# One of the four dBx products per scan state goes from VectorE to GpSimd, fed by a ScalarE copy of the B row

## The chip, the cores and the metric
One NeuronCore of a Trainium2 chip runs the whole program. The metric is the device time of one execution in microseconds (us), lower is better.

## The reference
The kernel computes two adaLN layers on 1024 tokens of width 512: a selective scan (Mamba style) with a routed LoRA feed-forward, then attention with an ALiBi bias and a quantised gated feed-forward. The change lies in the scan alone:

```
A   = -exp(A_log)                                  # 512 channels x 16 states
xp  = x @ x_proj_w.T ;  dt_in, B, C = split(xp)    # 16 | 16 | 16 per token
dt  = softplus(dt_in @ dt_proj_w.T + dt_proj_b)
dA  = exp(dt * A)
dBx = dt * B * x
h_t = dA_t * h_{t-1} + dBx_t                       # over 1024 tokens
y_t = sum over the 16 states of h_t * C_t ;  y = y + D * x
```

## The kernel before
Channels lie on the 128 partitions, in four blocks c = 0..3; tokens lie along the free dimension and are done in two halves h of 512. Within a half the 16 states follow one another; N = 16h + n counts them through. A helper, scan_turns, gives every engine the same loop: the first pair of states written out, six pairs in a hardware loop, the last pair written out (o = 0, 1 is the state within the pair). The engines are ordered by semaphores only, each in the order of its own program. For one state:

- TensorE broadcasts the row B (L623, PSUM bank 5) and the row C (L627, bank 4) of 512 tokens over all partitions. In its program the two broadcasts for state N+1 stand behind the hC matmul of channel block 0 of state N and ahead of that of block 1 (L645 to L650). The hC matmuls (L649, f32, against an identity, each recorded as two) add hC up over the states in banks 0 to 3. The broadcast of B waits until VectorE has done all four dBx products of the state before, that of C until C has been copied.
- ScalarE copies C to SBUF (L492, C_sb, two buffers), then computes dA of the four blocks as an exponential (L496) into banks 6 and 7 in turn; the exponential of block c waits for the scan that freed its bank, two blocks earlier.
- VectorE forms dBx = u * B of each block (L986, u from SBUF, B from PSUM, dBx to SBUF), one block ahead of the scan, and scans the block: hs = dA * hs + dBx (L1006). In its order: dBx c+1, scan c. In the first half of the tokens it also copies the last column of hs to a small tile, state (L990, keep_state); in the second half the scan starts from that.
- GpSimd multiplies hC = hs * C (L410), a block at a time, behind the scan. It waits for the hC matmul of the state before, which frees the buffer.

A scan of block c writes over hs of the state before, so it waits for GpSimd's hC of that block (`hc_done`).

Of the kernel before, what the change touches and what calls it, by code (L numbers as in the profile page):

```python
# [18 lines left out]
P = 128  # L19
# [72 lines left out]
def program(nc, a, out):  # L92
    ctx = ExitStack()
    with ctx:
# [60 lines left out]
        sp_exp = at("sp_exp", RG + 8, [P, DC, HALF])  # L155
        sp_w = at("sp_w", RG + 16, [P, DC, HALF])
        dBx = at("dBx", RG + 8, [P, DC, HALF])
        hs = at("hs", RG, [P, DC, HALF])
        hC = at("hC", RG + 16, [P, DC, HALF])
        C_sb = at("C_sb", RG + 24, [P, 2, HALF])  # L160
# [62 lines left out]
        for n in ("in_c in_x in_id in_misc in_l0 in_lf in_attn in_proj in_gate in_up in_down wd_p0 wd_p1 wd_p2 wd_r0 wd_r1 in_att "  # L223
                  "c_exp c_silu mod_acc mod_prod mod_mm mod_done mod_rest negA setup "
                  "ln_ve ln_rstd ln_norm ln_tr ln_hT "
                  "xp_mm xp_dt xp_bc dt_mm sp_e sp_w sp_act sp_lo sp_dve sp_free "
                  "b_mm c_mm c_evac da_done dbx_done scan_done st_done hc_done sum_done y_done ym yt "
                  "x0 ar_mm r_soft r_exp hw_done hw_tr hw_evac f0_mm f0_y x1 x1pre bias0 "
                  "qk_mm qk_evac qk_split v_mm v_done "
                  "s_mm m_done r_part rec_done r_rdy rt_mm rt_evac st_mm exp_done pv_done ot_evac ot_tr ao_done v_ones "  # L230
                  "aot_tr aot_evac pj_mm pj_y x2 x2pre bias1 "
                  "g_mm f_exp f_sgn f_y0 f_out dn_mm dn_y0 dn_sgn dn_y dn_done out_dma dchain pchain achain").split():
            sem(n)
# [128 lines left out]
        @block.gpsimd  # L362
        def _(pool):
            n = [0]

            def link(ins):
                n[0] += 1
                ins.then_inc(S["pchain"], 1)
                pool.wait_ge(S["pchain"], n[0])

            pool.memset(ones[:], 1.0).then_inc(S["setup"], 1)
            pool.memset(zb[:], 0.0).then_inc(S["setup"], 1)
            pool.memset(state[:], 0.0).then_inc(S["setup"], 1)
            link(pool.memset(mhalf[:], -0.5))

            def ln_rstd(l, h):
                pool.wait_ge(S["ln_ve"], 2 * l + h + 1)
                pool.tensor_tensor(rstd[:, 4 * h:4 * h + 4], veps[:, 4 * h:4 * h + 4], mhalf[:, 0:4], ALU.pow) \  # L378
                    .then_inc(S["ln_rstd"], 1)

            def pre_add(l, s, row):
                for t in range(NT):
                    pool.wait_ge(S["ln_norm"], NT * l + t + 1)
                    pool.tensor_tensor(x_tok[:, t, :], x_tok[:, t, :], row, ALU.add).then_inc(S[s], 1)

            ln_rstd(0, 0)
            ln_rstd(0, 1)

            for i in range(2 * DC):
                h, c = i // DC, i % DC  # L390
                if c == 0:
                    for c_ in range(DC):
                        pool.wait_ge(S["sp_e"], DC * h + c_ + 1)
                        pool.tensor_tensor(uT[:, c_, half(h)], sp_exp[:, c_, :], uT[:, c_, half(h)], ALU.subtract) \
                            .then_inc(S["sp_lo"], 1)
                pool.wait_ge(S["sp_dve"], i + 1)
                link(pool.tensor_tensor(dtT[:, c, half(h)], dtT[:, c, half(h)], sp_log[:, c, :], ALU.add))
                pool.tensor_tensor(uT[:, c, half(h)], dtT[:, c, half(h)], hT[:, c, half(h)], ALU.mult) \
                    .then_inc(S["sp_free"], 1)
            pool.wait_ge(S["sp_free"], 2 * DC)  # L400

            def scan(h, m, first_, last):
                for o in range(2):
                    N = m * 2 + (16 * h + o)
                    pool.wait_ge(S["c_evac"], N + 1)
                    for c in range(DC):
                        pool.wait_ge(S["scan_done"], N * DC + (c + 1))
                        if not (first_ and o == 0):
                            pool.wait_ge(S["sum_done"], N * DC + (c - 3))
                        pool.tensor_tensor(hC[:, c, :], hs[:, c, :], C_sb[:, o, :], ALU.mult) \  # L410
                            .then_inc(S["hc_done"], 1)

            scan_turns(pool, scan)
            ln_rstd(1, 0)
            ln_rstd(1, 1)
            pool.wait_ge(S["bias0"], 16 * 5 + 1)
            pre_add(1, "x1pre", bbc[:])

            pool.wait_ge(S["mod_prod"], 2)
            link(pool.tensor_tensor(wmod[:, 0, :], wmod[:, 0, :], wmod[:, 1, :], ALU.add))  # L420
            pool.wait_ge(S["mod_prod"], DC)
            link(pool.tensor_tensor(wmod[:, 2, :], wmod[:, 2, :], wmod[:, 3, :], ALU.add))
            pool.tensor_tensor(wmod[:, 0, :], wmod[:, 0, :], wmod[:, 2, :], ALU.add).then_inc(S["mod_acc"], 1)
            ln_rstd(2, 0)
            ln_rstd(2, 1)
            pool.wait_ge(S["x1"], NT)
            pool.memset(V[:, :, :, HD:32], 1.0).then_inc(S["v_ones"], 1)
            pool.wait_ge(S["bias1"], 16 * 2 + 1)
            pre_add(2, "x2pre", bpc[:])

            ln_rstd(3, 0)
            ln_rstd(3, 1)

            for i in range(IC + 1):
                for part, k in ((0, i), (1, i - 1)):
                    if 0 <= k < IC:
                        M = M_of(k)
                        pool.wait_ge(S[f"wd_p{part}"], k + 1)
                        pool.tensor_tensor(wd[0:M, k, :], wd[0:M, k, :], wdp[0:M, part, k, :], ALU.subtract) \
                            .then_inc(S[f"wd_r{part}"], 1)  # L440
# [3 lines left out]
        def _(act):  # L444
# [38 lines left out]
            act.wait_ge(S["sp_free"], 2 * DC)  # L483
            act.wait_ge(S["negA"], 2)

            def scan(h, m, first_, last):
                for o in range(2):
                    N = m * 2 + (16 * h + o)
                    act.wait_ge(S["c_mm"], N + 1)
                    if not first_:  # L490
                        act.wait_ge(S["hc_done"], N * DC - 4)
                    A_(C_sb[:, o, :], ps[:, C_BANK, :], ACT.Copy).then_inc(S["c_evac"], 1)  # L492
                    for c in range(DC):
                        if not (first_ and o == 0 and c < 2):
                            act.wait_ge(S["scan_done"], N * DC + (c - 1))
                        A_(ps[:, DA_BANK + c % 2, :], dtT[:, c, half(h)], ACT.Exp,  # L496
                           scale=nA[:, bass.ds(m * 2 + (o + c * NS), 1)]).then_inc(S["da_done"], 1)

            scan_turns(act, scan)
            ln_out(1, 0, 3, 4)  # L500
# [75 lines left out]
        def _(pe):  # L576
# [42 lines left out]

            def broadcast(h, n, guarded):  # L620
                if guarded:
                    pe.wait_ge(S["dbx_done"], n * DC + 16 * h * DC)
                mm(ps[:, B_BANK, :], sel[:, bass.ds(n, 1)].to_broadcast([96, P]), BCs[:, half(h)],  # L623
                   start=True, stop=True).then_inc(S["b_mm"], 1)
                if guarded:
                    pe.wait_ge(S["c_evac"], n + 16 * h)
                mm(ps[:, C_BANK, :], sel[:, bass.ds(n + NS, 1)].to_broadcast([96, P]), BCs[:, half(h)],  # L627
                   start=True, stop=True).then_inc(S["c_mm"], 1)
# [240 lines left out]
        def _(v):  # L869
# [109 lines left out]
            def scan(h, m, first_, last):  # L979
                def driven(o, c):  # L980

                    N = m * 2 + (16 * h + o)
                    v.wait_ge(S["b_mm"], N + 1)
                    if not (first_ and o == 0):
                        v.wait_ge(S["scan_done"], N * DC + (c - 3))
                    tt(dBx[:, c, :], uT[:, c, half(h)], ps[:, B_BANK, :], ALU.mult).then_inc(S["dbx_done"], 1)  # L986
# [9 lines left out]
                for o in range(2):  # L996
                    N = m * 2 + (16 * h + o)
                    for c in range(DC):
                        if not (last and o == 1 and c == DC - 1):
                            driven(o + (c + 1) // DC, (c + 1) % DC)  # L1000
                        v.wait_ge(S["da_done"], N * DC + (c + 1))
                        v.wait_ge(S["dbx_done"], N * DC + (c + 1))
                        if not (first_ and o == 0):
                            v.wait_ge(S["hc_done"], N * DC + (c - 3))
                        init = 0.0 if h == 0 else state[:, bass.ds(m * 2 + (o + c * NS), 1)]
                        v.tensor_tensor_scan(hs[:, c, :], ps[:, DA_BANK + c % 2, :], dBx[:, c, :], init,  # L1006
                                             ALU.mult, ALU.add).then_inc(S["scan_done"], 1)
                        if before and h == 0:
                            keep_state(*before)
                        before = (o, c)  # L1010
# [307 lines left out]
```

## Time and profile before
| | us |
|---|---|
| median of 3 runs | 1123.4 (1119.11 to 1123.93) |
| the profiled execution | 1121.76 |
| its span | 1120.0 |
| first half of the scan | about 118 to 242 |
| second half of the scan | about 255 to 371 |

Over the whole span TensorE's matmuls are busy 878.5 us (78%), VectorE 832.2 (74%), ScalarE 418.6 (37%), GpSimd 283.3 (25%). These shares are means over stages with different limits. In the rows below PE is TensorE's matmul, PEld its weight load, DVE is VectorE, ACT is ScalarE, POOL is GpSimd. An instruction's name is its source line with what it writes and reads. A start and an end come from the hardware profiler; the ends of matmuls are modelled.

### The profile page before, as it was taken

The numbers are of one execution on the slowest core, as the hardware profiler recorded it, in microseconds if no ns is written. First come the engines' busy times: TensorE is split into PE (matmuls) and PEld (weight loads), VectorE is DVE, ScalarE is ACT, GpSimd is POOL, SyncE is SP. The second block draws the span as 40 slices with busy tenths as digits, with TensorE's granted clock in tenths as the row PEclk, the third lists the DMA queues.
The fourth block names the chain that finished last, engine by engine and source line by source line (L and its number), as shares of the span: only waits on it lengthen the run. The fifth ranks groups of instructions, "written<-read, shape, count | busy, mean of one in ns | idle before, by whom it ended". The sixth has DMA issues, their size and how long they took to land.

```text
span 1120.0 us, 12563 instructions
## 1 busy us (share of the span) xinstructions
PE 878.5 (78%) x4157; PEld 404.6 (36%) x4166; DVE 832.2 (74%) x1307; ACT 418.6 (37%) x691; POOL 283.3 (25%) x210
## 2 busy tenths in 40 slices
PE   1750577656766583879759999999998889999997
PEld 1320122222111361434335555555544344444443
DVE  5299899989999757629359887778740639976777
ACT  0421344424444150022100666666675045543300
POOL 1135566645777290113000000000000014400000
PEclk9855699998999886979969999999999999999999
DMA  9314000000000000413420122222005000000010
GB/s 358 123 49 176 1 0 0 0 0 1 0 0 0 17 1 0 148 27 127 147 79 19 57 65 65 65 65 63 6 2 195 8 1 0 1 0 1 1 38 37
DMA packets 28797, 54.37 MB, mean 49 GB/s; under 512 B 7956, under 2 KB 14868, under 8 KB 27592
## 3 DMA queue, kind: packets, MB, share of 16 engines
q1 hardware_dynamic: 28744, 53.68, 14.2%
q8 instruction: 31, 0.51, 0.2%
q14 instruction: 22, 0.18, 0.1%
HBM read 45.08 MB, written 8.39 MB: 48 GB/s over the span
## 4 chain that ended last, share of the span: by engine, by line
PE 52%; DVE 9%; SPq 2%; issue 2%; ACT 1%; DMA 1%; POOL 0%; DVEq 0%; POOLq 0%
PE ps L852 14%; PE ps L776 7%; PE ps L758 5%; PE ps L863 5%; PE ps L740 3%; PE ps L745 3%; PE ps L834 2%; PE ps L795 2%; SPq L267 2%; PE ps L583 1%; PE ps L761 1%; PE ps L678 1%; PE ps L743 1%; PE ps L672 1%; DVE qkf L1125 1%
## 5 line engine op out<-in xcount | busy, mean ns | idle before, releaser
L532 ACT ACTIVATE prob<-ps 128x512 f32<-128x512 f32 x288 | 160.3, 600 | 141.1 <-PE ps L761 113.3
L649 PE MATMUL ps<-hC,identf 128*128 128x512 f32 x256 | 151.6, 682 | 73.8 <-POOL hC L410 72.3
L410 POOL TENSOR_TENSOR hC<-hs,C_sb 128x512 f32<-128x512 f32 x128 | 162.4, 1270 | 94.0 <-DVE hs L1006 73.3
L378 POOL TENSOR_TENSOR rstd<-veps,mhalf 128x4 f32<-128x4 f32 x8 | 10.4, 1294 | 459.0 <-DVE veps L890 459.0
L496 ACT ACTIVATE ps<-dtT,nA 128x512 f32<-128x512 f32 x128 | 88.2, 690 | 101.6 <-DVE hs L1006 101.6
L1142 DVE TENSOR_REDUCE mrow<-ps 128x4 f32<-128x512 f32 x160 | 103.1, 686 | 23.4 <-PE ps L743 12.2
L758 PE MATMUL ps<-stack 123*128 123x512 bf16 (+3 forms) x384 | 113.0, 327 | 0.6 <-ACT prob L532 0.3
L649 PEld LDWEIGHTS ps<-hC,identf 128*128 128x128 f32 x256 | 42.3, 201 | 166.9 <-POOL hC L410 163.7
L1145 DVE TENSOR_REDUCE mrow<-ps 128x1 f32<-128x512 f32 x128 | 82.0, 685 | 24.7 <-PE ps L745 24.7
L986 DVE TENSOR_TENSOR dBx<-uT,ps 128x512 f32<-128x512 f32 x128 | 86.6, 678 | 7.4 <-PE ps L623 4.8
L740 PE MATMUL ps<-stack 120*128 120x128 bf16 x640 | 73.8, 222 | 19.7 <-DVE mrow L1142 16.3
L852 PE MATMUL ps<-hT,wg 128*128 128x512 f32 (+1 forms) x176 | 80.9, 603 | 3.0 <-ACT hT L463 3.0
L1006 DVE TENSOR_TENSOR_SCAN hs<-ps,state,dBx 128x512 f32<-128x512 f32 x64 | 82.5, 1291 | 0.0
L776 PE MATMUL ps<-prob,V 128*32 128x512 f32 (+3 forms) x768 | 81.6, 498 | 0.7 <-ACT prob L532 0.7
L852 PE MATMUL ps<-hT,wu 128*128 128x512 f32 (+1 forms) x176 | 79.1, 592 | 0.0
L1006 DVE TENSOR_TENSOR_SCAN hs<-ps,dBx 128x512 f32<-128x512 f32 x64 | 77.9, 1218 | 0.3 <-ACT ps L496 0.3
L740 PEld LDWEIGHTS ps<-stack 120*128 120x128 bf16 x640 | 51.6, 99 | 62.7 <-DVE mrow L1142 37.9
L463 ACT ACTIVATE hT<-ps,modc 128x512 f32<-128x512 f32 x32 | 22.3, 776 | 109.4 <-PE ps L583 99.3
L710 PE MATMUL ps<-hT,wattn 128*128 128x512 f32 x128 | 58.8, 620 | 3.5 <-ACT hT L463 3.0
L863 PE MATMUL ps<-wdp,inter 128*128 128x512 bf16 (+1 forms) x258 | 56.7, 379 | 0.3
L583 PE MATMUL ps<-identf,xn 128*128 128x128 f32 x128 | 25.4, 374 | 32.6 <-DVE xn L897 32.5
L852 PEld LDWEIGHTS ps<-hT,wg 128*128 128x128 f32 (+1 forms) x176 | 33.5, 191 | 45.8 <-issue 45.8
(185 smaller groups left out, 1366.6 us busy)
## 6 DMA issues: line engine op xcount, KB each, us to landing
wmod<-in_wmod SPq DMA_DIRECT2D x8, 1536.0 KB, 13.6
stack<-parts_dram SPq DMA_DIRECT2D x192, 64.0 KB
parts_dram<-qkp SPq DMA_DIRECT2D x48, 128.0 KB, 1.8
wattn<-in_wattn SPq DMA_DIRECT2D x1, 3072.0 KB, 13.3
wg<-in_wg SPq DMA_DIRECT2D x1, 2752.0 KB, 9.3
wu<-in_wu SPq DMA_DIRECT2D x1, 2752.0 KB, 10.7
wd<-in_wd SPq DMA_DIRECT2D x1, 2560.0 KB, 12.7
x_tok<-in_x SPq DMA_DIRECT2D x1, 2048.0 KB, 8.0
```

Source lines behind the costliest of these rows:

```text
L410: pool.tensor_tensor(hC[:, c, :], hs[:, c, :], C_sb[:, o, :], ALU.mult) \
L496: A_(ps[:, DA_BANK + c % 2, :], dtT[:, c, half(h)], ACT.Exp, scale=nA[:, bass.ds(m * 2 + (o + c * NS), 1)]).then_inc(S["da_done"], 1)
L532: A_(prob[:, u % 4, j, :], ps[:, 3 + F % 3, :], ACT.Exp).then_inc(S["exp_done"], 1)
L649: mm(ps[:, c, :], identf[:], hC[:, c, :], start=False, stop=False, skip_group_check=True).then_inc(S["sum_done"], 1)
L740: ins = mm(ps[:, bank, tile(j_)], qk[0:ATT_S, 0, j_, tile(i)], qk[0:ATT_S, 1, j_, tile(kb)], start=True, stop=kb < i)
L758: ins = mm(ps[:, bank, col:col + w], qk[0:ATT_ALL, 1, j, tile(kb)], qk[0:ATT_ALL, 0, j, q0:q0 + w], start=True, stop=not diag)
L776: ins = mm(ps[32 * j:32 * j + 32, 6 + b, q0 % HALF:q0 % HALF + w], V[:, kb, g * GH + j, :], prob[:, U % 4, j, col:col + w], start=(kb == 0 ...
L852: ins = mm(ps[0:M, 2 * s + b, :], w[:, k, ib * P:ib * P + M], hT[:, k, half(h)], start=(k == 0), stop=(k == DC - 1))
L863: ins = mm(ps[:, 4 + t % 4, :], inter[0:M, k, tile(t)], wdp[0:M, part, k, :], start=(k == 0 and part == 0), stop=(k == IC - 1 and part == 2))
L986: tt(dBx[:, c, :], uT[:, c, half(h)], ps[:, B_BANK, :], ALU.mult).then_inc(S["dbx_done"], 1)
L1006: v.tensor_tensor_scan(hs[:, c, :], ps[:, DA_BANK + c % 2, :], dBx[:, c, :], init, ALU.mult, ALU.add).then_inc(S["scan_done"], 1)
L1142: v.reduce_max(mrow[:, kb, :, i], ps[:, bank, :].rearrange("p (j c) -> p j c", c=P), AX) \
```

## The change
The kernel gets two more SBUF buffers of 128 x 512 f32: a second buffer for the dBx of block 3 (dB3 alternates between it and the old one) and B_sb, a copy of the B row. The steps:

- ScalarE copies the B row of state N+1 from PSUM to B_sb, between its exponentials of blocks 2 and 3 of state N (and the row of state 0 of each half first of all). It waits for the broadcast and until GpSimd has used the row before. It signals `b_evac`.
- GpSimd forms dBx of block 3 of state N+1 from B_sb, between its hC products of blocks 1 and 2 of state N (and that of state 0 of each half first of all). It waits for `b_evac` and signals `dbx3_done`.
- VectorE forms dBx of blocks 0 to 2 only, still from PSUM, but waits for `b_evac` in place of the broadcast. Its order in a state is now dBx 1, scan 0, dBx 2, scan 1, scan 2, dBx 0 of the next state, scan 3.
- TensorE's broadcast of B waits for the three dBx products of the state before and for the copy of its row.

```diff
+        dB3 = [dBx[:, DC - 1, :], at("dB3", RG + 28, [P, HALF])[:]]
+        B_sb = at("B_sb", 30, [P, HALF])
@@ GpSimd
+            def driven(h, N, o):
+                pool.wait_ge(S["b_evac"], N + 1)
+                pool.tensor_tensor(dB3[o], uT[:, DC - 1, half(h)], B_sb[:], ALU.mult).then_inc(S["dbx3_done"], 1)
             def scan(h, m, first_, last):
+                if isinstance(m, int) and m == 0:
+                    if h:
+                        pool.wait_ge(S["scan_done"], 16 * DC)
+                    driven(h, 16 * h, 0)
...
+                        if c == 1 and not (last and o == 1):
+                            driven(h, N + 1, 1 - o)
@@ ScalarE
+            def copy_b(N, read):
+                act.wait_ge(S["b_mm"], N + 1)
+                if read:
+                    act.wait_ge(S["dbx3_done"], N)
+                A_(B_sb[:], ps[:, B_BANK, :], ACT.Copy).then_inc(S["b_evac"], 1)
...
+                        if c == 2 and not (last and o == 1):
+                            copy_b(N + 1, True)
@@ TensorE, broadcast
-                    pe.wait_ge(S["dbx_done"], n * DC + 16 * h * DC)
+                    pe.wait_ge(S["dbx_done"], n * (DC - 1) + 16 * h * (DC - 1))
+                    pe.wait_ge(S["b_evac"], n + 16 * h)
@@ VectorE
-                    v.wait_ge(S["b_mm"], N + 1)
+                    v.wait_ge(S["b_evac"], N + 1)
...
-                        if not (last and o == 1 and c == DC - 1):
-                            driven(o + (c + 1) // DC, (c + 1) % DC)
+                        if c < DC - 2:
+                            driven(o, c + 1)
+                        elif c == DC - 1 and not (last and o == 1):
+                            driven(o + 1, 0)
...
-                        v.wait_ge(S["dbx_done"], N * DC + (c + 1))
+                        if c < DC - 1:
+                            v.wait_ge(S["dbx_done"], N * (DC - 1) + (c + 1))
+                        else:
+                            v.wait_ge(S["dbx3_done"], N + 1)
...
-                        v.tensor_tensor_scan(hs[:, c, :], ps[:, DA_BANK + c % 2, :], dBx[:, c, :], init,
+                        v.tensor_tensor_scan(hs[:, c, :], ps[:, DA_BANK + c % 2, :],
+                                             dBx[:, c, :] if c < DC - 1 else dB3[o], init,
```

## Rows read from the trace of the kernel before

**Rows 1.** Busy time of each engine by stretch; x counts, granted clock, DMA.

```profile
core 0: us, PE busy (x) PEld busy (x) DVE busy (x) ACT busy (x) POOL busy (x), PEclk, DMA share, GB/s
118.00:242.00 124.00, 87.03 (x162) 25.68 (x162) 115.40 (x192) 52.01 (x80) 81.26 (x64) 0.90 0.00 0
...
255.00:371.00 116.00, 80.69 (x158) 22.96 (x159) 113.52 (x128) 50.56 (x78) 81.84 (x65) 0.96 0.00 0
```

**Rows 2.** Groups by line in the scan: busy us, mean ns, idle before, releasers.

```profile
L410 POOL TENSOR_TENSOR hC<-hs,C_sb 128x512 f32<-128x512 f32 x128 | 162.4, 1270 | 94.0 <-DVE hs L1006 73.3 <-issue 18.0 <-PE ps L649 2.8
...
L986 DVE TENSOR_TENSOR dBx<-uT,ps 128x512 f32<-128x512 f32 x128 | 86.6, 678 | 7.4 <-PE ps L623 4.8 <-issue 2.3
...
L1006 DVE TENSOR_TENSOR_SCAN hs<-ps,dBx 128x512 f32<-128x512 f32 x64 | 77.9, 1218 | 0.3 <-ACT ps L496 0.3
...
L492 ACT ACTIVATE C_sb<-ps 128x512 f32<-128x512 f32 x32 | 19.1, 597 | 72.1 <-PE ps L627 58.4 <-POOL hC L410 13.7
```

**Rows 3.** Timeline, second half, one state: start, duration, engine, line, idle before.

```profile
299.13 1.28 DVE L1006 TENSOR_TENSOR_SCAN hs<-ps,state,dBx 128x512 f32<-128x512 f32 x1
...
306.22 1.29 DVE L1006 TENSOR_TENSOR_SCAN hs<-ps,state,dBx 128x512 f32<-128x512 f32 x1
...
307.42 0.67 DVE L986 TENSOR_TENSOR dBx<-uT,ps 128x512 f32<-128x512 f32 x1
...
307.67 1.27 POOL L410 TENSOR_TENSOR hC<-hs,C_sb 128x512 f32<-128x512 f32 x1 [0.57 <-DVE hs L1006]
308.00 1.29 DVE L1006 TENSOR_TENSOR_SCAN hs<-ps,state,dBx 128x512 f32<-128x512 f32 x1
...
309.00 1.12 PE L649 MATMUL ps<-hC,identf 128*128 128x512 f32 x2 [0.72 <-POOL hC L410]
309.19 0.68 DVE L986 TENSOR_TENSOR dBx<-uT,ps 128x512 f32<-128x512 f32 x1
...
310.00 0.39 PE L623 MATMUL ps<-BCs,sel 96*128 96x512 bf16 x1
...
310.96 0.68 DVE L986 TENSOR_TENSOR dBx<-uT,ps 128x512 f32<-128x512 f32 x1
```

**Rows 4.** Timeline of VectorE, first half, around two loop turns.

```profile
193.50 1.22 DVE L1006 TENSOR_TENSOR_SCAN hs<-ps,dBx 128x512 f32<-128x512 f32 x1
...
195.46 0.69 DVE L986 TENSOR_TENSOR dBx<-uT,ps 128x512 f32<-128x512 f32 x1 [0.45 <-issue]
196.07 1.22 DVE L1006 TENSOR_TENSOR_SCAN hs<-ps,dBx 128x512 f32<-128x512 f32 x1
...
210.98 1.22 DVE L1006 TENSOR_TENSOR_SCAN hs<-ps,dBx 128x512 f32<-128x512 f32 x1
```

**Rows 5.** Timeline, end of the first half.

```profile
236.82 1.22 DVE L1006 TENSOR_TENSOR_SCAN hs<-ps,dBx 128x512 f32<-128x512 f32 x1
...
237.99 1.22 DVE L1006 TENSOR_TENSOR_SCAN hs<-ps,dBx 128x512 f32<-128x512 f32 x1
238.12 2.49 POOL L410 TENSOR_TENSOR hC<-hs,C_sb 128x512 f32<-128x512 f32 x2 [0.50 <-DVE hs L1006]
```

**Rows 6.** Timeline, start of the first half, TensorE at half clock.

```profile
118.40 0.63 PE L627 MATMUL ps<-BCs,sel 96*128 96x512 bf16 x1
...
119.15 0.60 ACT L492 ACTIVATE C_sb<-ps 128x512 f32<-128x512 f32 x1 [30.21 <-PE ps L627]
119.64 1.29 ACT L496 ACTIVATE ps<-dtT,nA 128x512 f32<-128x512 f32 x2
120.36 1.22 DVE L1006 TENSOR_TENSOR_SCAN hs<-ps,dBx 128x512 f32<-128x512 f32 x1 [0.34 <-ACT ps L496]
...
121.75 1.27 POOL L410 TENSOR_TENSOR hC<-hs,C_sb 128x512 f32<-128x512 f32 x1 [7.81 <-DVE hs L1006]
...
123.08 2.07 PE L649 MATMUL ps<-hC,identf 128*128 128x512 f32 x2 [4.04 <-POOL hC L410]
...
124.94 0.63 PE L623 MATMUL ps<-BCs,sel 96*128 96x512 bf16 x1
...
125.61 0.69 DVE L986 TENSOR_TENSOR dBx<-uT,ps 128x512 f32<-128x512 f32 x1 [0.50 <-PE ps L623]
```

**Rows 7.** Waits in the scan: total us, times, longest.

```profile
DVE dBx L986 <- PE ps L623: 4.8, 6, 2.6
```

More of the change, by code:

```diff
@@ L226, in program @@
                   "xp_mm xp_dt xp_bc dt_mm sp_e sp_w sp_act sp_lo sp_dve sp_free "
-                  "b_mm c_mm c_evac da_done dbx_done scan_done st_done hc_done sum_done y_done ym yt "
+                  "b_mm c_mm c_evac b_evac da_done dbx_done dbx3_done scan_done st_done hc_done sum_done y_done ym yt "
                   "x0 ar_mm r_soft r_exp hw_done hw_tr hw_evac f0_mm f0_y x1 x1pre bias0 "
@@ L484, in _ @@
             act.wait_ge(S["negA"], 2)
+            def copy_b(N, read):
[3 more added lines that the diff above has]
+                A_(B_sb[:], ps[:, B_BANK, :], ACT.Copy).then_inc(S["b_evac"], 1)
             def scan(h, m, first_, last):
+                if isinstance(m, int) and m == 0:
+                    copy_b(16 * h, h > 0)
                 for o in range(2):
```

## The prediction
> **What bounds the kernel now.** The edit touches nothing outside the two scan stages, so I first read the busy times by stretch, to see who fills these stages. Over the first half VectorE is busy 115.4 of 124 us and GpSimd 81.3; over the second VectorE 113.5 of 116, GpSimd 81.8, ScalarE 50.6 [rows 1]. VectorE is the wall, all others have room. The groups of instructions by line then say what fills it: per state (16 states in each half) four dBx products of 0.68 us and four scans of 1.22; one GpSimd product takes 1.27, a ScalarE copy of a 512-column row 0.60 [rows 2].
>
> Busy times don't say what follows when VectorE gets shorter; for that I walked the timeline of one steady state [rows 3]. State to state, scan of channel 0 to scan of channel 0, is 306.22 - 299.13 = 7.09 us. The reader should see a second path beside VectorE: the B row is broadcast by one TensorE matmul (L623), which stands in TensorE's program behind the hC matmul of channel 0. That matmul needs GpSimd's hC of channel 0, and this needs scan 0 of the same state. The row is there at 310.00 + 0.39 = 310.39 and its first reader, the dBx of channel 0 of the next state, starts at 310.96. So this path has only 0.57 us to spare per state. Everything turns on that number.
>
> **What the change does to VectorE alone.** It removes 32 dBx products. Between two scans a product costs its issue distance: 0.58 (307.42 to 308.00 [rows 3]) or 0.61 us (195.46 to 196.07 [rows 4]); a scan with no product behind it costs 1.17 (236.82 to 237.99 [rows 5]). If nothing else were late, a state would take 7.09 - 0.60 = 6.49, and 32 states would give back 32 x 0.60 = 19 us. VectorE's busy time falls by 32 x 0.68 = 21.8 in any case.
>
> **What it adds on the B path.** ScalarE copies the B row before anybody may read it, and even VectorE's own products now wait for the end of that copy. The path, from GpSimd's start on hC of channel 0:
> - GpSimd hC: 1.27 [rows 2]; to the matmul 0.06 (307.67 + 1.27 = 308.94, 309.00 [rows 3]).
> - hC matmul until the broadcast starts. In the steady row it is 1.00 (309.00 to 310.00), but there the broadcast is released by the dBx of channel 3, which ended at 309.87; that condition goes earlier by the change. The bare distance shows where TensorE ran at half clock: 124.94 - 123.08 = 1.86 [rows 6]; half of it, 0.93, is my value at full clock. The far ends are nothing at all (if it were hidden) and 1.86; the nearest row bounds it at 1.00 from above, and below 0.93 nothing in the rows goes.
> - Broadcast 0.39 [rows 3]; to ScalarE 0.12 (118.40 + 0.63 = 119.03, 119.15 [rows 6]).
> - The copy 0.60 [rows 2]; to its reader 0.03 (exponential 119.64 + 0.69 = 120.33, scan 120.36 [rows 6]).
>
> Sum 1.27 + 0.06 + 0.93 + 0.39 + 0.12 + 0.60 + 0.03 = **3.40 us**. It closes into a ring in two ways. Through VectorE: dBx 0 of the next state, scan 3, dBx 1, scan 0 of the next state, GpSimd's next hC 0. With the second half's distances, 0.58 + 1.20 (306.22 to 307.42) + 0.58 and 1.45 from scan start to hC start (306.22 to 307.67 [rows 3]), the ring is 3.40 + 2.36 + 1.45 = 7.21. In the first half 0.61 + 1.17 + 0.61 + 1.39 (120.36 to 121.75 [rows 6]) gives 7.18. Through GpSimd: its dBx3, which also waits for the copy, then hC 2, hC 3 and the next hC 0, back to back at 1.22 to 1.27 each (two in 2.49 [rows 5]): 3.40 + 0.05 + 3.7 = 7.1 to 7.2. Behind the waiting dBx3 in GpSimd's queue stand hC 2 and hC 3, so their matmuls go later too, which costs nothing by itself. On ScalarE the exponential of channel 3 stands behind the waiting copy: it starts 0.49 after the copy's start (119.15 to 119.64 [rows 6]) and takes 0.69, so scan 3 can start 0.49 + 0.69 + 0.03 = 1.21 after the copy's start, against 0.60 + 0.03 + 0.58 = 1.21 through dBx 0: a tie. Three paths come out near 7.2, and the 0.60 that VectorE gets is eaten by the copy's 0.60 + 0.12 + 0.03 against a slack of 0.57.
>
> The GpSimd reference page of the Trainium skill (GPSIMD Engine Reference, section "Engine selection") advises against two-input elementwise work on GpSimd, as about twice as slow. The rows show 1.27 against 0.68, 1.9 times. By the page's factor the moved product would take 1.36 and the ring through GpSimd 7.3 at most.
>
> **Sum at full clock.** Second half: 7.21 - 7.09 = +0.12 x 15 = +1.8. First half: there each turn of the loop over two states has a pause on VectorE behind the last scan (193.50 to 195.46, 1.96 instead of 1.17, that is +0.79), and two states take 210.98 - 196.07 = 14.91 [rows 4]. After: 2 x 7.18 + 0.79 = 15.15, since the pause lies on the same ring; +0.24 x 7.5 = +1.8.
>
> **Low clock.** In low stretches TensorE shows 0.50, its 1.2 GHz level; the mean granted clock of 0.90 and 0.96 [rows 1] makes (0.10 / 0.5) x 124 = 24.8 and (0.04 / 0.5) x 116 = 9.3 us at that level, 4.8 states' worth. Now such a state costs little: VectorE waited for the broadcast 4.8 us in all, 2.6 of it once at the start [rows 7], so 2.2. Afterwards nothing covers it: 0.93 more for the hC matmul and 0.63 - 0.39 = 0.24 for the broadcast [rows 6], 1.17 x 4.8 = 5.6. Net +3.4. If TensorE falls behind in such a state (hC matmuls queue up), it is up to twice that; if the low stretches are no more than before and fall on other work, it is nothing.
>
> **Ends.** At the start of the first half the copy comes ahead of the first dBx: B row near 119.3, two products, scan 0 at about 120.6 instead of 120.36: +0.3. In the second half VectorE comes later than the row, so nothing. In the last state of each half no row is awaited. Before, hC 3 ended at 238.12 + 2.49 = 240.61, that is 7.33 after scan 0 (scan 2 at 236.82 [rows 5] less two steps of 7.09 / 4 = 1.77, so 233.28); after, hC 1 starts at 3.1 and three products run back to back to 6.8: -0.5 each, -1.0.
>
> Total +1.8 + 1.8 + 3.4 + 0.3 - 1.0 = **+6.3 us**. The profiled execution took 1121.8 (span 1120.0), so 1128.1 for it; it lies 1.6 below the median of the runs shown, 1123.4, so against that **1129.7**. Its SBUF costs (a buffer at an unused place) are nothing; no DMA is added or moved.
>
> **Bounds of what no row shows.** The handovers on the new path lie between 0.03 and 0.16 (scan end 307.51 to GpSimd 307.67) each, three of them new or now decisive: -0.15 to +0.25 per state, -5 to +8 in all. Clock: -2 to +7 around my term. A copy's true distance, 0.49 to 0.60, moves at most -3.
>
> **Rivals.**
> 1. Faster: the row comes in time and VectorE remains the wall at 6.49 a state: -19, with the clock's 3.4 on top some 1107. For it: VectorE is over 93% busy. Against: the row would have to come 0.7 us earlier than the rows allow; no part of the path but the waits can shrink, and they sum to 0.21. Chance 0.06.
> 2. Clearly slower: the ring carries more delay than the rows' best handovers, and low-clock states come with a backlog on TensorE. Four engines now hand over in one ring where one engine ran on; with 0.25 more per state (8) and the clock at twice its price (+3.4 more), +18: 1141. It decides from a ring of about 7.4. For it: three paths tie at 7.2, and whichever is late each time sets the step. Chance 0.24.
> 3. GpSimd and VectorE shut each other out while both read SBUF. In this kernel VectorE's product and scan take one tensor from PSUM and one from SBUF. Beside GpSimd's products the scans showed 1.22, and two scans back to back beside two products back to back took 1.17 and 2.49 [rows 5], no stretch. Were a fifth GpSimd product to hold VectorE up for its length once per state, it would be 1.27 x 32 = +41, 1165. Chance 0.02. The Trainium skill has this rule (SBUF — State Buffer, section "Who interferes with whom"): an instruction of VectorE with two SBUF inputs contends with a GpSimd one that reads SBUF, one with at most one doesn't. By it, this rival can't come, and the trace agrees.
>
> That the change doesn't do what it says I exclude: the products are moved in the program's order.
>
> **Chances and range.** My forecast holds with 0.68; what a measurement here can tell from no change is about 0.5%, 5.6 us, that is 1117.8 to 1129.0. My sum sits on the upper edge: within this case 0.36 same, 0.30 slower, 0.02 faster. Rival 1 adds 0.06 faster, rival 2 gives 0.02 same and 0.22 slower, rival 3 0.02 slower: 0.08, 0.38, 0.54. The range takes the lower bounds of handovers and clock, and rival 2 above: 1120 to 1144.
>
> **What would show it.** In the changed profile: VectorE's busy time 22 lower; its dBx of channel 0 waiting each state for ScalarE's copy, some 0.6 to 0.7 us; scan 2 directly behind scan 1 at 1.17; GpSimd near 6.35 of 7.2 us busy per state, its dBx3 waiting for the copy; steady state 7.1 to 7.3. Wrong if the dBx of channel 0 starts without a wait (rival 1), if scans or GpSimd products grow longer (rival 3), or if the ring measures over 7.4 at full clock (rival 2).

## The result and the profile after

The changed kernel took 1136.32 us (median of 4 runs, 1131.77 to 1137.15) against 1121.59 (4 runs) before: ratio 1.0124, 95% interval 1.0099 to 1.0149. It is slower, as forecast, and the range of 1120 to 1144 held it. The predicted 1129.7 was 6.6 us too low; as a change, the kernel lost 14.7 us where +6.3 was forecast, since the kernel before came out 1.8 us lower here than in the table above. The profiled execution took 1136.66 us (span 1134.8, against 1120.0).

Busy time by stretch, with the scan's two halves now at 118 to 244 and 260 to 382 (columns as in [rows 1]):

```profile
118.00:244.00 126.00, 86.90 (x155) 26.66 (x155) 106.77 (x176) 58.53 (x96) 98.88 (x80) 0.86 0.00 0
260.00:382.00 122.00, 85.33 (x155) 27.08 (x156) 105.18 (x112) 57.38 (x94) 98.93 (x80) 0.87 0.00 0
```

VectorE's busy time fell and the stretches grew. It fell by 8.6 and 8.3 us in these stretches, less than the forecast 22, although the rows of dBx alone went from 86.6 to 64.7: neighbouring instructions overlap in the record (the product of 307.42 in [rows 3] lasts 0.67, yet the scan starts 0.58 behind its start), so that a product less frees about 0.6 us and not 0.68. From first dBx to the end of the last scan the first half took 124.85 us (before 120.47); from first to last scan the second took 120.50 (before 112.94). Their sum is 11.9 us longer, of 14.8 in the whole span; the start and the time between the halves add 0.3, and 2.6 lie behind the scan, where the kernels of this study scatter by as much (749 to 754 us from the last scan's end to the end). The second thing to see is the granted clock: 0.86 and 0.87 where it had been 0.90 and 0.96.

The groups that answer to [rows 2]:

```profile
L421 POOL TENSOR_TENSOR hC<-hs,C_sb 128x512 f32<-128x512 f32 x126 | 158.2, 1267 | 25.6 <-DVE hs L1035 21.8 <-issue 1.3 <-PE ps L673 1.0
...
L1010 DVE TENSOR_TENSOR dBx<-uT,ps 128x512 f32<-128x512 f32 x96 | 64.7, 675 | 37.1 <-ACT B_sb L503 34.5 <-issue 2.4
...
L407 POOL TENSOR_TENSOR dBx<-uT,B_sb 128x512 f32<-128x512 f32 x16 | 20.3, 1272 | 29.7 <-ACT B_sb L503 29.7
...
L503 ACT ACTIVATE B_sb<-ps 128x512 f32<-128x512 f32 x32 | 19.1, 597 | 121.0 <-PE ps L647 121.0
```

No instruction of VectorE, GpSimd or ScalarE has grown longer: GpSimd's products take 1.27, VectorE's 0.68, the copy 0.60. What is new is VectorE's idle time ahead of dBx, 34.5 us for the copy. The waits of VectorE, for [rows 7]:

```profile
DVE dBx L1010 <- ACT B_sb L503: 34.5, 31, 3.3
```

A full-clock state of the second half, for [rows 3]:

```profile
280.94 1.27 POOL L407 TENSOR_TENSOR dB<-uT,B_sb 128x512 f32<-128x512 f32 x1 [0.34 <-ACT B_sb L503]
280.99 0.69 DVE L1010 TENSOR_TENSOR dBx<-uT,ps 128x512 f32<-128x512 f32 x1 [0.64 <-ACT B_sb L503]
...
282.16 3.91 POOL L421 TENSOR_TENSOR hC<-hs,C_sb 128x512 f32<-128x512 f32 x3
...
283.37 1.28 DVE L1035 TENSOR_TENSOR_SCAN hs<-ps,state,dBx 128x512 f32<-128x512 f32 x1
...
283.49 2.35 PE L673 MATMUL ps<-hC,identf 128*128 128x512 f32 x4 [1.72 <-POOL hC L421]
...
285.14 2.45 DVE L1035 TENSOR_TENSOR_SCAN hs<-ps,state,dBx 128x512 f32<-128x512 f32 x2
...
286.13 1.13 PE L673 MATMUL ps<-hC,identf 128*128 128x512 f32 x2 [0.29 <-POOL hC L421]
...
287.09 0.38 PE L647 MATMUL ps<-BCs,sel 96*128 96x512 bf16 x1
...
287.51 0.60 ACT L503 ACTIVATE B_sb<-ps 128x512 f32<-128x512 f32 x1 [2.04 <-PE ps L647]
...
288.18 1.27 POOL L407 TENSOR_TENSOR dBx<-uT,B_sb 128x512 f32<-128x512 f32 x1 [0.34 <-ACT B_sb L503]
288.24 0.69 DVE L1010 TENSOR_TENSOR dBx<-uT,ps 128x512 f32<-128x512 f32 x1 [0.65 <-ACT B_sb L503]
```

From dBx 0 to dBx 0 it is 288.24 - 280.99 = 7.25 us. The path can be read downwards: hC 0 on GpSimd, the last of the three products from 282.16 on, ends near 286.07, its matmul starts at 286.13, the broadcast at 287.09, the copy at 287.51, and GpSimd's dBx 3 (288.18) and VectorE's dBx 0 (288.24) both start on the copy's end. VectorE waited 0.65 for it. The two scans 1 and 2 stand back to back (the row of 285.14 is both). TensorE meanwhile stood still for 1.72 before 283.49, because GpSimd did dBx 3 (280.94) first and hC 2 only from 282.16 on.

A state in which TensorE ran at half clock (the granted clock is 0.50 for 3.4 us of it):

```profile
190.50 4.83 PE L673 MATMUL ps<-hC,identf 128*128 128x512 f32 x6 [1.77 <-POOL hC L421]
...
193.53 1.26 POOL L421 TENSOR_TENSOR hC<-hs,C_sb 128x512 f32<-128x512 f32 x1 [0.51 <-DVE hs L1035]
...
195.13 0.49 PE L647 MATMUL ps<-BCs,sel 96*128 96x512 bf16 x1
...
195.66 0.60 ACT L503 ACTIVATE B_sb<-ps 128x512 f32<-128x512 f32 x1 [3.23 <-PE ps L647]
...
196.39 0.69 DVE L1010 TENSOR_TENSOR dBx<-uT,ps 128x512 f32<-128x512 f32 x1 [1.80 <-ACT B_sb L503]
```

Here hC 2, hC 3 and hC 0 are one unbroken row of matmuls from 190.50; GpSimd was through with hC 0 before 193.53, where it begins hC 1, yet the broadcast comes at 195.13 and VectorE waits 1.80 instead of 0.65. Two turns of the loop in the first half, for [rows 4]:

```profile
157.66 0.69 DVE L1010 TENSOR_TENSOR dBx<-uT,ps 128x512 f32<-128x512 f32 x1 [0.65 <-ACT B_sb L503]
...
164.85 0.69 DVE L1010 TENSOR_TENSOR dBx<-uT,ps 128x512 f32<-128x512 f32 x1 [0.61 <-ACT B_sb L503]
...
167.43 0.69 DVE L1010 TENSOR_TENSOR dBx<-uT,ps 128x512 f32<-128x512 f32 x1 [0.46 <-issue]
...
172.84 0.69 DVE L1010 TENSOR_TENSOR dBx<-uT,ps 128x512 f32<-128x512 f32 x1 [0.66 <-ACT B_sb L503]
```

From 157.66 to 172.84 are 15.18 us for two states, 7.19 and 7.99.

### The profile page after: what moved, and what is told of

It reads as the page before. It is cut to its first block, busy times and chain, and to the rows that moved or that the text cites. A ratio compares the mean times of both kernels' runs of the same rounds, so it can differ in the third digit from the quotient of the medians.

```text
span 1134.8 us, 12700 instructions
## 1 busy us (share of the span) xinstructions
PE 891.0 (79%) x4157; PEld 412.6 (36%) x4166; DVE 817.1 (72%) x1275; ACT 431.4 (38%) x723; POOL 320.8 (28%) x242
## 4 chain that ended last, share of the span: by engine, by line
PE 51%; DVE 9%; SPq 2%; issue 1%; ACT 1%; DMA 1%; POOL 0%; DVEq 0%; POOLq 0%
PE ps L876 14%; PE ps L800 7%; PE ps L782 5%; PE ps L887 5%; PE ps L764 3%; PE ps L769 3%; PE ps L858 2%; PE ps L819 2%; SPq L269 2%; PE ps L606 1%; PE ps L702 1%; PE ps L785 1%; PE ps L767 1%; DVE qkf L1155 1%; PE ps L696 1%
## 5 line engine op out<-in xcount | busy, mean ns | idle before, releaser
L673 PE MATMUL ps<-hC,identf 128*128 128x512 f32 x256 | 163.0, 740 | 76.7 <-POOL hC L421 73.3
L673 PEld LDWEIGHTS ps<-hC,identf 128*128 128x128 f32 x256 | 47.9, 218 | 175.7 <-POOL hC L421 167.3
L1010 DVE TENSOR_TENSOR dBx<-uT,ps 128x512 f32<-128x512 f32 x96 | 64.7, 675 | 37.1 <-ACT B_sb L503 34.5
L1035 DVE TENSOR_TENSOR_SCAN hs<-ps,state,dBx 128x512 f32<-128x512 f32 x56 | 69.9, 1272 | 0.0
L1035 DVE TENSOR_TENSOR_SCAN hs<-ps,dBx 128x512 f32<-128x512 f32 x56 | 67.5, 1216 | 0.0
L503 ACT ACTIVATE B_sb<-ps 128x512 f32<-128x512 f32 x32 | 19.1, 597 | 121.0 <-PE ps L647 121.0
```

The source lines that it names most:

```text
L673: mm(ps[:, c, :], identf[:], hC[:, c, :], start=False, stop=False, skip_group_check=True).then_inc(S["sum_done"], 1)
```

## The experiments

Ratios are to the kernel before, with 95% intervals. The theory on record was a ring through hC 0, broadcast and copy, plus the low clock; its rivals were GpSimd as the limit and a clock that is no cause. "Row first" means the broadcasts moved ahead of the matmul of hC 0. The diffs are cut to the lines that matter. A clock or a row is that of the one profiled execution of each kernel; the times are medians.

**The copy alone**, on the kernel before.
```diff
+                            copy_b(N + 1, True)    # ScalarE, behind the exponential of block 2
...
+                    pe.wait_ge(S["b_evac"], n + 16 * h)    # TensorE, before the broadcast
...
-                    v.wait_ge(S["b_mm"], N + 1)
+                    v.wait_ge(S["b_evac"], N + 1)
```


> The kernel before plus ScalarE's copy of the B row and the wait for it on VectorE and TensorE; VectorE still forms all four dBx products and nobody reads the copy. Ring theory (the step is set by hC 0, its matmul, the broadcast, the copy, dBx 0, scan 3, dBx 1, scan 0): the ring is the same as in the changed kernel, so 7.2 us per state at full clock, about 1.2 more in a low-clock state, ratio to before 1.010 to 1.015. GpSimd theory (its fifth product is what makes the changed kernel slow): ScalarE is half idle, ratio 0.998 to 1.003.

1129.52 us, ratio 1.0053 (1.0036 to 1.0070). GpSimd does its old four products here, so its fifth product isn't needed for a loss; but the size is half of what I expected, a miss. One step at full clock:

```profile
279.84 0.69 DVE L996 TENSOR_TENSOR dBx<-uT,ps 128x512 f32<-128x512 f32 x1 [0.20 <-ACT B_sb L489]
...
285.19 0.66 DVE L996 TENSOR_TENSOR dBx<-uT,ps 128x512 f32<-128x512 f32 x1
...
286.07 0.39 PE L633 MATMUL ps<-BCs,sel 96*128 96x512 bf16 x1
...
286.49 0.60 ACT L489 ACTIVATE B_sb<-ps 128x512 f32<-128x512 f32 x1 [2.18 <-PE ps L633]
...
287.23 0.69 DVE L996 TENSOR_TENSOR dBx<-uT,ps 128x512 f32<-128x512 f32 x1 [0.19 <-ACT B_sb L489]
```

Here VectorE's dBx 3 (285.19, ends 285.85) releases the broadcast, and the step is 287.23 - 279.84 = 7.39, even longer than 7.25. So this ring is not the one expected: it runs through dBx 3, the broadcast, the copy and dBx 0. The run shows that the copy costs on the way of the B row; that hC 0 is in the changed kernel's ring is shown by "row first" below. What is missing for the full loss is the low clock: the granted clock is 0.93 in the first and 0.96 in the second half, and only 4 waits of VectorE, besides the first, exceed 0.9 us, against 13 in the changed kernel. A longer step alone, then, didn't bring the low clock here.

**Zero matmuls that keep TensorE busy**, in the changed kernel and in the one before.
```diff
+                        if c:
+                            for _ in range(2):
+                                mm(ps[:, c, :], zb[:, 0:P], zb[:], start=False, stop=False, skip_group_check=True)
```


> The changed kernel with two more 512-column matmuls of zeros behind the hC matmul of channel blocks 1, 2 and 3, added to the sums, to keep TensorE busy. Clock theory: of the 14.7 us lost about 10 are low-clock states, whose waits of VectorE for the copy are 1.3 to 1.8 us instead of 0.65. With the clock at 1.00 after the first states only the full-clock step of 7.2 is left: ratio 1.003 to 1.006. If the clock is a companion and no cause: ratio 1.012 or more.

1125.73 us, ratio 1.0038 (1.0022 to 1.0054), the granted clock:

```profile
118.00:239.00 121.00, 91.80 (x246) 32.26 (x246) 106.57 (x176) 58.55 (x96) 98.61 (x79) 0.96 0.00 0
256.00:372.00 116.00, 90.56 (x246) 32.42 (x247) 105.00 (x112) 57.24 (x94) 98.51 (x80) 0.97 0.00 0
```

> The kernel before with the same zero matmuls. Clock theory: before, the low clock cost VectorE only some 2 us of waits, so ratio 0.997 to 1.000. If TensorE's clock acted on the scan in some other way, it would gain here too, 0.990 to 0.995.

1123.21 us, ratio 1.0003 (0.9989 to 1.0017). So 0.86 points of the changed kernel's 1.24, some 9.7 us (by the two intervals 6 to 13), are the low clock, though extra work was added. In the profiled executions the two scans got 10.2 us shorter by it (245.3 to 235.1), and those of the kernel before, where the path had cover, 1.6 (233.4 to 231.8), which its median doesn't show. In the filled kernel only 2 waits, besides the first, exceed 0.9 us: 1.71 and 1.67, in the first state of each half.

**dBx 3 behind hC 2** instead of hC 1 on GpSimd, else the changed kernel.
```diff
-                        if c == 1 and not (last and o == 1):
+                        if c == 2 and not (last and o == 1):
                             driven(h, N + 1, 1 - o)
```


> The changed kernel with GpSimd's dBx of block 3 placed behind its hC 2 instead of behind hC 1; same instructions, same ring through VectorE (3.44 + 2.38 + 1.43 = 7.25 us at full clock). In the changed kernel TensorE stands still 1.7 to 1.8 us per state before the hC matmul of block 2, since GpSimd first waits for the copy and forms dBx 3. Pause theory (that standstill is what brings the low clock more often): the pause is split into shorter ones, the granted clock in the scan comes back from 0.86 towards 0.93, ratio 1.004 to 1.009. If where TensorE stands still does not matter: clock 0.86 and ratio 1.011 to 1.014 again.

1130.26 us, ratio 1.0059 (1.0039 to 1.0078).

```profile
118.00:242.00 124.00, 82.28 (x154) 25.21 (x154) 106.70 (x176) 58.08 (x96) 98.75 (x80) 0.91 0.00 0
258.00:376.00 118.00, 80.58 (x155) 24.07 (x156) 105.24 (x112) 57.51 (x95) 98.48 (x80) 0.94 0.00 0
```

The clock is 0.91 and 0.94, and half of the loss is gone, with the same instructions and the same full-clock step: dBx 0 at 300.85 and again at 308.09, 7.24 us, with waits of 0.65 and 0.64 for the copy. The longest standstill of a full-clock state is 1.33 instead of 1.72 us. The profiled execution, 1126.58, is one of the two faster of five; over the whole program the mean granted clock of the five is 0.904 to 0.913, that of the changed kernel's four 0.885 to 0.901. So where TensorE stands still matters.

**The kernel before with one long standstill.** The matmul of hC 1 waits until hC 2 is there.
```diff
-                        pe.wait_ge(S["hc_done"], N * DC + (c + 1))
+                        pe.wait_ge(S["hc_done"], N * DC + (3 if c == 1 else c + 1))
```


> The kernel before, with the hC matmul of block 1 waiting until hC 2 is there too, so that TensorE stands still about 1.8 us once per state (as it does in the changed kernel) and then does two blocks at once. No instruction is added or taken away, and VectorE's ring is not touched. Pause theory (one long standstill per state is what brings the low clock more often): the granted clock in the scan falls from 0.90 and 0.96 to 0.88 or less; the time rises little, 1.001 to 1.005, since the broadcast is covered at half clock up to 0.57 us. If the low clock of the changed kernel comes from its longer step or from GpSimd: clock as before, 0.90 to 0.96, and ratio 0.998 to 1.002.

1126.66 us, ratio 1.0042 (1.0023 to 1.0060). Busy time and clock, then TensorE's matmuls around the standstill:

```profile
118.00:240.00 122.00, 84.54 (x155) 29.63 (x155) 115.24 (x192) 52.00 (x80) 80.78 (x64) 0.83 0.00 0
255.00:370.00 115.00, 82.33 (x150) 29.55 (x150) 111.41 (x127) 51.34 (x79) 77.33 (x61) 0.81 0.00 0
```

```profile
305.24 0.38 PE L627 MATMUL ps<-BCs,sel 96*128 96x512 bf16 x1
307.56 4.84 PE L649 MATMUL ps<-hC,identf 128*128 128x512 f32 x7 [1.94 <-POOL hC L410]
```

The clock fell from 0.90 and 0.96 [rows 1] to 0.83 and 0.81 by this alone: TensorE waits 1.94 us before it does two blocks at once. Neither GpSimd's fifth product nor a copy is in this kernel. The profiled execution is the slowest of the six and has the lowest clock, 0.877 over the whole program; the other five have 0.888 to 0.894, the kernel before 0.905 to 0.923 in nine. So a longer standstill in each state, with two blocks done at once behind it, brings the low clock by itself. VectorE's waits for the broadcast grew from 4.8 [rows 7] to 8.1 us, 3.3 us of the 4.5 by which the two scans are longer in this execution (237.9 against 233.4): the price stays small while the broadcast has its cover of 0.57 us.

**Row first**, in the changed kernel.
```diff
-                        if c == 1 and not (last and o == 1):
+                        if c == 0 and not (last and o == 1):
                             broadcast(h, m * 2 + (1 + o), True)
```


> The changed kernel with the two broadcasts for the next state placed ahead of the hC matmul of channel block 0 instead of behind it. Ring theory: hC 0 and its matmul leave the ring, the row is there about 1.3 us earlier, VectorE is the wall again at 6.49 us per state (GpSimd needs at least 5 x 1.25 = 6.25), so about 19 us less than before: ratio 0.980 to 0.987. GpSimd theory: GpSimd's five products keep the step near 7.2 or more, ratio 1.005 to 1.015.

1104.57 us, ratio 0.9829 (0.9812 to 0.9845). One state:

```profile
280.33 0.38 PE L647 MATMUL ps<-BCs,sel 96*128 96x512 bf16 x1
...
280.75 0.60 ACT L503 ACTIVATE B_sb<-ps 128x512 f32<-128x512 f32 x1 [1.00 <-PE ps L647]
280.76 1.02 PE L673 MATMUL ps<-hC,identf 128*128 128x512 f32 x2
...
281.80 0.65 DVE L1010 TENSOR_TENSOR dBx<-uT,ps 128x512 f32<-128x512 f32 x1
```

and the next broadcast:

```profile
286.82 0.38 PE L647 MATMUL ps<-BCs,sel 96*128 96x512 bf16 x1
```

The broadcast (280.33) comes ahead of the matmul of hC 0 (280.76), the copy at 280.75, and dBx 0 follows at 281.80 without a wait. From broadcast to broadcast the step is 286.82 - 280.33 = 6.49. That is the wall of the prediction's first part to the hundredth, and the kernel is 19 us faster than the one before, as much as the change seemed to promise. GpSimd, with five products in 6.49 us, holds it, so GpSimd as the limit is ruled out. The total agrees in part by luck: each half's first state takes 1.2 us less than before, twice the 0.6, and four states at low clock take 0.8 to 1.0 more than their neighbours, such as the one that ends with this wait:

```profile
295.79 0.69 DVE L1010 TENSOR_TENSOR dBx<-uT,ps 128x512 f32<-128x512 f32 x1 [0.94 <-ACT B_sb L503]
```

**Row first in the kernel before.** Same edit.

> The kernel before (four products on VectorE, no copy) with the broadcasts ahead of the hC matmul of block 0. Ring theory: VectorE is the wall at 7.09 with or without it, and here the broadcast even has to wait for dBx 3 of its state, which holds the matmul of hC 0 up beside VectorE; ratio 0.998 to 1.004. If the order alone were worth something (less waiting at low clock): 0.995 to 0.998. The gain of the kernel with the row first then needs both the order and the move.

1117.66 us, ratio 0.9950 (0.9933 to 0.9966): a miss, it gains more than I gave it. The broadcast now waits for the dBx of block 3, and TensorE with it:

```profile
283.58 0.66 DVE L986 TENSOR_TENSOR dBx<-uT,ps 128x512 f32<-128x512 f32 x1
...
284.37 0.39 PE L623 MATMUL ps<-BCs,sel 96*128 96x512 bf16 x1 [1.74 <-DVE dBx L986]
```

TensorE stands still 1.74 us, and the clock of the first half falls to 0.85, yet no wait of VectorE for the broadcast is left but the first, where there were 2.2 us [rows 7]. The two halves of the scan took 118.24 and 112.37, together 2.8 us less than before; the first state of each half alone gives 1.2 of it (7.04 and 7.09 instead of 7.63 and 7.65). Of the 4.1 us by which the spans of the two profiled executions differ, 1.6 lie ahead of the scan, where the edit changes nothing and the first dBx of the kernels of this study starts between 117.1 and 119.0. So only the part in the scan is explained. Every state of the second half took 7.09 us at a mean clock of 0.93: low clock without a path that depends on it costs nothing.

**Row first and VectorE reading the copy**: its three products take B from SBUF.
```diff
-                    tt(dBx[:, c, :], uT[:, c, half(h)], ps[:, B_BANK, :], ALU.mult)
+                    tt(dBx[:, c, :], uT[:, c, half(h)], B_sb[:], ALU.mult)
...
+                    act.wait_ge(S["dbx_done"], N * (DC - 1))    # ScalarE, before the copy
```


> The kernel with the row first (ratio 0.983), with VectorE's three products reading the copy in SBUF in place of PSUM, so that they have two inputs in SBUF while GpSimd reads SBUF. Contention theory (one waits until the other's instruction ends): VectorE is the wall here, and up to 1.2 us per product and state show on VectorE or GpSimd, ratio 1.0 or more, with instructions that last longer than 0.68 or 1.27 or waits ahead of them. Without contention: 0.982 to 0.986, the product perhaps 0.02 us longer.

1150.48 us, ratio 1.0245 (1.0228 to 1.0262), 46 us more than with PSUM as the source. Two pairs of starts:

```profile
283.25 0.69 DVE L1010 TENSOR_TENSOR dBx<-uT,B_sb 128x512 f32<-128x512 f32 x1 [1.71 <-ACT B_sb L504]
283.30 1.77 POOL L407 TENSOR_TENSOR dBx<-uT,B_sb 128x512 f32<-128x512 f32 x1 [0.55 <-ACT B_sb L504]
```

```profile
291.68 1.27 POOL L407 TENSOR_TENSOR dB<-uT,B_sb 128x512 f32<-128x512 f32 x1 [0.62 <-ACT B_sb L504]
291.73 1.77 DVE L1010 TENSOR_TENSOR dBx<-uT,B_sb 128x512 f32<-128x512 f32 x1 [1.87 <-ACT B_sb L504]
```

In the first pair VectorE starts 0.05 us ahead, takes 0.69, and GpSimd's product lasts 1.77 instead of 1.27. In the second GpSimd starts ahead, takes its 1.27, and VectorE's lasts 1.77 instead of 0.68: it ends 0.55 after GpSimd's. Whoever comes second ends nearly as late as if it had been held until the first was through (0.13 us earlier in either pair). The Trainium skill (SBUF — State Buffer, section "Who interferes with whom") says that a VectorE instruction with two SBUF inputs contends with a GpSimd one that reads SBUF, and that the order of issue decides who is blocked; the trace agrees. GpSimd's hC products took 1.51 on average, VectorE's dBx 0.88. Two more things are in the 46 us: the extra wait on ScalarE (TensorE's broadcast no longer waits for VectorE, in its place), and the granted clock, which fell to 0.78 and 0.85; I didn't part the three.

**Two refinements of row first.**

> The kernel with the row first and the zero matmuls behind the hC matmuls of blocks 1 to 3. In the kernel with the row first VectorE waited for the copy at low clock in one place only, so the clock costs it almost nothing: ratio 0.981 to 0.984, the same as without the filler. If the low clock still cost it 3 us or more elsewhere (hC buffers freed late): 0.978 to 0.980.

1104.33 us, ratio 0.9828 (0.9812 to 0.9845): the same as without the zero matmuls. That doesn't show that the clock is worth nothing here. In the profiled executions the long states of row first (7.42 to 7.53 in the second half) are gone, 3.8 us in all, but now every second state there takes 6.71 instead of 6.49, so that the added work costs some 2.5 us of it again.

> The kernel with the row first, and GpSimd's dBx of block 3 behind hC 2. VectorE is the wall at 6.49 per state and GpSimd is nearly full (5 x 1.25); ratio 0.981 to 0.985, the same as with the row first alone. If GpSimd's order mattered at this step: hC 3 follows scan 3 without a product ahead of it, 0.978 to 0.980.

1102.62 us, ratio 0.9838 (0.9818 to 0.9858); by the ratios not told apart from row first alone. In the profiled executions its scans are 3.8 us shorter (211.1 against 214.9), at a clock of 0.96 and 0.97 against 0.93 and 0.91, and all 15 steps of the second half are 6.49.

## Why the prediction was right, and where its size was off

**The cover of 0.57 us decides: right.** The copy of 0.60 with two handovers used it up, and VectorE's 32 spared products of 0.60 were waited away. The copy alone made the kernel slower without any product moved, and the row-first kernel gave the 19 us back. The slack is also the most that the move could have given in this order: with 0.57 to spare in 7.09, the path itself takes 6.52 us, so with no copy at all the step could have shrunk by 0.57 at best.

**The ring of 3.40 us: right, with two handovers off that cancel.** At full clock it measured 1.27 + 0.06 + 0.96 + 0.38 + 0.04 + 0.60 + 0.13 = 3.44 from GpSimd's hC 0 to dBx 0 (predicted 0.93 for the matmul of hC 0 and 0.39 for the broadcast). The handover to the copy took 0.04 where 0.12 was predicted, that from the copy to its reader 0.13 where 0.03 was; that they nearly cancel is luck. The step was 7.25 against 7.21, and two states of the first half 15.18 against 15.15. The other two branches tie with it, as predicted. GpSimd's hC 0 starts at 284.80, with scan 0 ended at 284.65 and GpSimd's hC 3 at 284.66. ScalarE's exponential of block 3 ended 0.14 ahead of scan 3.

**The full-clock sum of +3.6, with the ends +2.9: about right.** In the scans of the changed kernel with zero matmuls 1.7 us are left over those of before (120.13 + 114.98 against 120.47 + 112.94), and by its ratio 4.3 us of the whole. With zero matmuls in both kernels the scans differ by 3.3 us (235.1 against 231.8). Of these 1.2 are the first state of each half, 8.2 to 8.3 us instead of 7.6, for which the prediction had only 0.3.

**The low clock, +3.4: the term that was mis-sized.** The price of one such state was right: a wait of 1.80 instead of 0.65 is 1.15 more, against 1.17 predicted. Their number was not. The granted clock of 0.86 and 0.87 makes (0.14 / 0.5) x 126 + (0.13 / 0.5) x 122 = 67 us at half clock, 9.2 states' worth instead of 4.8; at the predicted price that is 10.8 us, less the 2.2 of before +8.6. VectorE's waits for the copy, without the first, sum to 31.2 us; 30 waits of 0.63 would be 18.9, so 12.3 are the low clock, 10.1 over the 2.2 that it cost before. The zero matmuls took back 9.7. I had carried the share of low clock over from the kernel before and only priced it anew; the text's own upper bound, +7 around the term, would have held 10.4. What I did not see is that GpSimd's fifth product, put between hC 1 and hC 2, makes TensorE stand still 1.7 us in every state, and that this lowers the clock. I had written that the matmuls of hC 2 and hC 3 "go later too, which costs nothing by itself", and that sentence is what failed. Two kernels show it from both sides: the product behind hC 2 took back 7 of 14 us, and a standstill alone lowered the clock of the kernel before to 0.83 and 0.81. That the range held the result, with a change more than twice the forecast one, is owed to its upper end, which came from rival 2.

**VectorE's busy time "22 lower in any case": wrong, about 17**, as read above. The sum went by 0.60 per product and is not touched by it.

**The rivals.** Faster (0.06) did not come, but it is what the ring hid, and one moved line brings it. Clearly slower (0.24) came near in size, +18 against 14.7. It put 8 of them on slow handovers, and these summed to what the rows had; its other half, a backlog on TensorE and the clock at twice its price, did come. Contention (0.02) did not come since VectorE reads B from PSUM; with B from SBUF it is there.

## What to carry to other kernels

Before relieving the busiest engine, measure the slack of every path that must close once per step, and take from it what the relief adds; 0.57 us of slack against 0.75 of new latency decided this case, not 22 us of busy time. That slack is also the most that the step can shrink while the path stays as it is. A broadcast or load for the next step belongs in its engine's program ahead of the work that waits for this step's result. And a change that makes TensorE's idle time one long piece instead of several short ones can lower its clock, which costs most where TensorE is on the ring; a faster step can put it there again, as the four long states of row first show.

## What was not expected of the hardware

A standstill of 1.9 us per state of 7.1, with no less work, took the granted clock from 0.90 and 0.96 to 0.83 and 0.81; in the changed kernel one of 1.7 went with 0.86 and 0.87, and one of 1.33 with 0.91 and 0.94. The length of the longest piece doesn't settle the clock: one of 1.33 also went with 0.93 and 0.91 in row first and with 0.96 and 0.97 when dBx 3 stood behind hC 2 there, and 1.74 with 0.93 in the second half of the kernel before with the row first. What besides decides it stays open. At half clock the matmuls of three blocks queue up (six in 4.83 us), so that a state also pays for the blocks ahead. Of a VectorE product with both inputs in SBUF and a GpSimd product that start 0.05 us apart, the second lasts 1.77 us, instead of 0.68 or 1.27.
